# First attention's tail: SyncE issues all loads, the last x goes straight to its place, scatters begin between the last heads, no shared unit in the routing

## What is computed

```python
h  = cond_attn(x, fside, mask)            # layernorm, 16 heads over 513 keys, causal, bias, layernorm
x1 = x + head_mix(h)                      # per token: softmax over the 16 heads of the same token, @ Wout + bout
# mixture of experts with 8 experts, top 2, and a shared expert
scores = softmax((x1 @ wt.T + g @ wg.T) / 2)
w, idx = top_k(scores, 2)
y  = sum_k(w_k * expert[idx_k](x1)) + (leaky(x1 @ sw_gate) * (x1 @ sw_up)) @ sw_down
out = x1 + ffn(y)                         # a second attention, layernorms, and a mixture with 8 experts, top 1
```

## Time and profile before

| What | Value |
|---|---|
| median of 3 runs | 2566.62 us (2559.79 to 2570.12) |
| the profiled execution's own time | 2564.33 us |
| its span, first to last instruction | 2562.5 us |
| mean granted TensorE clock | 0.935 |
| busy share: PE, DVE, ACT, POOL | 83%, 58%, 46%, 40% |
| DMA, mean | 68 GB/s |

### The profile page before, as it was taken

How to read it: one execution, slowest core, us unless ns; L and a number is a source line. 1 busy time by engine, 2 the same in 40 slices (tenths; PEclk the granted TensorE clock), 3 DMA queues, 4 the chain that set the end, 5 groups by cost and what they waited for, 6 DMA issues and landing times.

```text
span 2562.5 us, 33680 instructions
## 1 busy us (share of the span) xinstructions
PE 2136.9 (83%) x11656; PEld 1152.8 (45%) x11656; DVE 1483.5 (58%) x3123; ACT 1174.8 (46%) x2748; POOL 1015.0 (40%) x790
## 2 busy tenths in 40 slices
PE   2999999999898988855857948899999988835995
PEld 1555555555555655522426823233333323313764
DVE  1346767786868686758423437666676664313336
ACT  0776666666666665611112421455555545401221
POOL 0105656574747484733365521102221011243216
PEclk9999999999999999978888977999999999857998
DMA  7002222221100000020434522111111502014214
GB/s 234 10 34 78 79 80 79 70 87 66 58 18 10 10 5 13 5 87 1 129 127 150 157 82 59 41 32 54 44 54 38 183 17 71 17 41 144 64 53 134
DMA packets 149647, 173.98 MB, mean 68 GB/s; under 512 B 18633, under 2 KB 132809, under 8 KB 149226
## 3 DMA queue, kind: packets, MB, share of 16 engines
q1 hardware_dynamic: 85226, 81.32, 10.2%
q10 hardware_dynamic: 49712, 50.79, 5.8%
q0 software_dynamic: 14544, 39.73, 5.0%
HBM read 86.98 MB, written 80.61 MB: 65 GB/s over the span
## 4 chain that ended last, share of the span: by engine, by line
PE 58%; POOL 12%; DVE 11%; ACT 8%; issue 5%; ACTq 2%; DMA 2%; SPq 1%; POOLq 0%; DVEq 0%
PE ps L1767 11%; POOL prod L815 7%; ACT m_pt L1895 6%; PE ps L574 3%; PE ps L547 3%; PE ps L533 3%; PE ps L558 3%; PE ps L584 3%; PE ps L2111 3%; PE ps L2119 3%; PE ps L1778 3%; DVE sc L827 3%; PE ps L1733 3%; DVE pb L698 2%; PE ps L1211 2%
## 5 line engine op out<-in xcount | busy, mean ns | idle before, releaser
L1832 DVE TENSOR_REDUCE m_mx<-ps 128x2 f32<-128x1024 f32 x256 | 312.4, 1224 | 178.2 <-PE ps L1751 177.2
L1895 ACT ACTIVATE m_pt<-ps 128x1024 f32<-128x1024 f32 x256 | 262.0, 1023 | 310.0 <-PE ps L1767 310.0
L698 DVE CUSTOM_DVE_ANT_0 pb<-ps,bias,snl 128x128 f32<-128x128 f32 (+3 forms) x512 | 260.4, 546 | 226.4 <-PE ps L547 223.6
L815 POOL TENSOR_TENSOR prod<-qs,kvs 128x1024 f32<-128x1024 f32 x120 | 285.1, 2403 | 224.9 <-issue 132.8
L1767 PE MATMUL ps<-m_q,m_k 32*128 32x512 f32 x1024 | 294.3, 651 | 52.2 <-ACT m_pt L1895 44.0
L815 POOL TENSOR_TENSOR prod<-sc,kvs 128x1024 f32<-128x1024 f32 x120 | 280.8, 2373 | 112.5 <-ACT sc L933 91.3
L1751 PE MATMUL ps<-m_k,m_q 32*128 32x512 f32 x1024 | 290.1, 666 | 5.2 <-DVE m_mx L1832 5.1
L893 ACT ACTIVATE pb<-pb,mst 128x129 f32<-128x129 f32 (+3 forms) x512 | 283.4, 560 | 21.1 <-DVE mst L698 19.1
L547 PE MATMUL ps<-kz,qT 64*128 64x128 f32 (+3 forms) x1024 | 185.3, 440 | 0.0
L558 PE MATMUL ps<-ident,pb 128*128 128x128 f32 x1280 | 180.0, 280 | 0.5 <-DVE mst L698 0.4
L1914 POOL DMA_INDIRECT m_yg<-ye_scratch,e_pos x64 | 63.4, 991 | 284.4 <-DVE m_x L1820 248.1
(11 more groups left out here) (326 smaller groups left out, 3773.9 us busy)
## 6 DMA issues: line engine op xcount, KB each, us to landing
xe_scratch<-zt ACTq DMA_DIRECT2D x32, 1024.0 KB, 4.5
ye_scratch<-e_ys SPq DMA_DIRECT2D x36, 256.0 KB, 2.1
hw_w<-in_w SPq DMA_DIRECT2D x16, 512.0 KB, 5.7
ys_scratch<-h_ys SPq DMA_DIRECT2D x39, 128.0 KB, 1.7
xin<-in_x SPq DMA_DIRECT2D x8, 512.0 KB, 3.6
bias<-in_fside ACTq DMA_DIRECT2D x8, 512.0 KB, 11.6
xr<-in_x SPq DMA_DIRECT2D x32, 128.0 KB, 2.3
y_scratch<-e_y SPq DMA_DIRECT2D x8, 512.0 KB, 3.2
```

The costliest lines, as they stand in the source:

```text
L698: dv.tensor_tensor_reduce(pb.ap[:, j, SEG[t]:SEG[t] + n], rS.of(("S", b, p, t, j)).ap[:, 0:n], k.bias[:, h, CAUSAL[t]:CAUSAL[t + 1]], -1.0 ...
L815: e.tensor_tensor(out, one, two, ALU.mult).then_inc(*k.c.did(*product_done(step, b, t, u)))
L1832: dv.tensor_reduce(x.ap[:, t, 64 * half:64 * half + 64].rearrange("p (i r) -> p i r", i=2)[:, :, 16], k.qS.of((b, g, t, half)).ap, AX, ALU ...
L1895: ac.activation(p.ap[:, 2 * half:2 * half + 2, :], k.qE.of((b, g, kt, half)).ap, ACT.Exp).then_inc(*did("m_exp", b, g, kt, half))
```

## The change

SP takes over all loads that ACT issued in `e_weights` and `mha_load`. A new step `x_last`, right behind `e_weights`, loads the four x tiles of batch 7 straight into their places in `e_x`; POOL adds the bias to all four at once, and `turn_o` of batch 7 no longer loads or adds on SP and POOL; `x1` adds in place. `e_load` stands before the heads `two` instead of behind them. In `two` there are nine shared units (n = 0, 1, 2, 4, 5, 6, 8, 9, 10) instead of six (n = 0, 2, 4, 6, 8, 10), and one tile's scatters behind n = 7 and behind n = 9. In batch 7's routing one shared unit is left instead of five, before its `count`. The transposes and scores of batch 7 use the PSUM banks of the ring `rM`.

```diff
+        elif step == "x_last":
+            for t in range(NT):
+                sp.dma_start(x1_tile(k, NB - 1, t), ins["x"][NB - 1, t * P:(t + 1) * P, :]).then_inc(*did("d_xl", t))
+        elif step == "turn_o" and key[0] < NB - 1:
...
-            x = k.xr.of((b, t))
+            x = x1_tile(k, b, t)
             w.wait_ge(at("wout", b, t), at("xb", b, t))
-            dv.tensor_tensor(x1_tile(k, b, t), rM.of(("x1", b, t)).ap[:, 0:D], x.ap[:, :], ALU.add).then_inc(*did("x1", b, t))
+            dv.tensor_tensor(x, rM.of(("x1", b, t)).ap[:, 0:D], x, ALU.add).then_inc(*did("x1", b, t))
...
+        elif step == "x_last":
+            w.wait_ge(at("d_xl", NT - 1))
+            for t in range(NT):
+                x = x1_tile(k, NB - 1, t)
+                po.tensor_tensor(x, x, k.bout[:, :], ALU.add).then_inc(*did("xb", NB - 1, t))
...
-    out = [("e_weights",)] + [x for part in start for x in part]
+    rows = [("scatter", n) for n in range(*LOT[0])]
+    share = iter([("shared", i) for i in range(2 * NB + 2)])
+    out = [("e_weights",), ("x_last",)] + [x for part in start for x in part]
...
-    out += turns
-    chain, i = routes(0), 0
+    out += turns + [("e_load",)]
+    chain = routes(0)
     for n, part in enumerate(two):
         out += part + chain[:1]
         chain = chain[1:]
-        if n % 2 == 0:
-            out.append(("shared", i))
-            i += 1
-    out += chain + [("e_load",)]
+        if n % 4 != 3:
+            out.append(next(share))
+        if n > 6 and n % 2:
+            out.append(rows.pop(0))
+    out += chain
     for part in end:
-        out += part + [("shared", i)]
-        i += 1
-    out += [("scatter", n) for n in range(*LOT[0])]
+        out += part + [next(share)]
+    out += rows
     b = NB - 1
-    for x in [("r_turn", b), ("r_score", b), ("r_back", b)] + routes(1):
-        out.append(x)
-        if x[0] in ("r_turn", "r_back", "r_soft", "r_rank", "r_cnt"):
-            out.append(("shared", i))
-            i += 1
-    return out + [("scatter", n) for n in range(*LOT[1])] + [("slots",)] + [("shared", j) for j in range(i, 2 * NB + 2)]
+    out += [("r_turn", b), ("r_score", b), ("r_back", b)] + routes(1)[:-1] + [next(share), ("count", 1)]
+    return out + [("scatter", n) for n in range(*LOT[1])] + [("slots",)] + list(share)
...
+def route_ring(k, b):
+
+    return k.rR if b < NB - 1 else k.rM
...
 def sync_two(k, sp, w, order):
...
+    def load(name, i, dst, src):
+        sp.dma_start(dst, src).then_inc(*did("d_" + name, i))
...
 def scalar_two(k, ac, w, order):
...
-    def load(name, i, dst, src):
-        ac.dma_start(dst, src).then_inc(*did("d_" + name, i))
...
-ONE = frozenset("turn_h lat q2 kv2 hs hs_soft hs_sum hv hv_end turn_o x1".split())
+ONE = frozenset("x_last turn_h lat q2 kv2 hs hs_soft hs_sum hv hv_end turn_o x1".split())
```

More of the change, by code:

```diff
@@ L969, in gpsimd_one @@
                 product(k, po, w, step, b, t, u)
-        elif step == "turn_o":
+        elif step == "x_last":
[3 more added lines that the diff above has]
+                po.tensor_tensor(x, x, k.bout[:, :], ALU.add).then_inc(*did("xb", NB - 1, t))
+        elif step == "turn_o" and key[0] < NB - 1:
             b, t = key
@@ L1095, in pairs_of @@
     return slice(2 * j * P, 2 * (j + 1) * P)
+def route_ring(k, b):
+    return k.rR if b < NB - 1 else k.rM
 def sync_two(k, sp, w, order):
     did, ins = k.c.did, k.ins
+    def load(name, i, dst, src):
+        sp.dma_start(dst, src).then_inc(*did("d_" + name, i))
     for step, *key in order:
-        if step == "e_load":
+        if step == "e_weights":
+            load("router", 0, cols(k.wt), ins["moe_wt"].rearrange("(c p) e -> p c e", p=P))
+            load("router", 1, cols(k.wg), ins["moe_wg"])
+            load("router", 2, cols(k.cT), ins["condT"][:, 0:NB])
+            load("router", 3, cols(k.before), ins["c_before"])
+            for b in range(NB - 1):
+                w.wait_ge([at(f"d_x1_{t % 2}", b, t) for t in range(NT)])
+                load(f"ex1_{b}", 0, k.ex1[:, b * NT:(b + 1) * NT, :], k.x1d[b * NT:(b + 1) * NT].rearrange("t p d -> p t d"))
+            load("shared", 0, cols(k.sg), ins["sh_gate"].rearrange("(c p) m -> p c m", p=P))
+            load("shared", 1, cols(k.su), ins["sh_up"].rearrange("(c p) m -> p c m", p=P))
+            load("shared", 2, cols(k.sd), ins["sh_down"].rearrange("(c p) m -> p c m", p=P))
+            load("tables", 0, cols(k.upper), ins["c_upper"])
+            load("tables", 1, cols(k.thr), ins["c_thr"][:, 0:2 * NN])
+            load("tables", 2, cols(k.iota), ins["c_iota"][:, 0:NS_E])
+            load("tables", 3, cols(k.place), ins["c_place"])
+        elif step == "mha_load":
+            load("mw", 0, cols(k.mwqk), ins["wi_qk"].rearrange("(c p) n -> p c n", p=P))
+            load("mw", 7, cols(k.mwv), ins["wi_v"].rearrange("(c p) n -> p c n", p=P))
+            load("mw", 1, cols(k.mbqk), ins["bi_qk"])
+            load("mw", 2, cols(k.mbv), row(ins["bi"][2 * D:3 * D]))
+            load("mw", 3, cols(k.mwo), ins["wo2"].rearrange("(c p) n -> p c n", p=P))
+            load("mw", 4, cols(k.mbo), row(ins["bo2"]))
+            load("mw", 5, cols(k.mg1), row(ins["ln1_g"]))
+            load("mw", 6, cols(k.mb1), row(ins["ln1_b"]))
+            w.wait_ge(at("d_yd0", 0))
+            load("m_x0", 0, cols(k.mx), k.yd[0:NT].rearrange("t p d -> p t d"))
+        elif step == "e_load":
             for x in range(E8):
@@ L1138, in tensor_two @@
             b = key[0]
-            m = k.rR.take(("score", b), at("e_lgT", b))
+            m = route_ring(k, b).take(("score", b), at("e_lgT", b))
             w.wait_ge(at("e_xT", b, 1), at("d_router", 3), m.room)
@@ L1437, in scalar_two @@
 def scalar_two(k, ac, w, order):
-    did, ins = k.c.did, k.ins
-    def load(name, i, dst, src):
-        ac.dma_start(dst, src).then_inc(*did("d_" + name, i))
+    did = k.c.did
     for step, *key in order:
[L1444 to L1459, removed]
+        if step == "r_init":
             w.wait_ge(at("e_cs", 0))
@@ L1465, in scalar_two @@
                 w.wait_ge(at("e_tr", b, c))
-                ac.activation(k.exT[:, b, c, :], k.rR.of(("turn", b, c)).ap, ACT.Copy).then_inc(*did("e_xT", b, c))
+                ac.activation(k.exT[:, b, c, :], route_ring(k, b).of(("turn", b, c)).ap, ACT.Copy).then_inc(*did("e_xT", b, c))
         elif step == "r_score":
@@ L1470, in scalar_two @@
             w.wait_ge(at("e_lg", b), at("e_csc", 0), l.room)
-            ac.activation(l.ap[:, :], k.rR.of(("score", b)).ap[0:E8, :], ACT.Identity, bias=k.cs[:, b:b + 1], scale=0.5).then_inc(*did("e_lgT", b))
+            ac.activation(l.ap[:, :], route_ring(k, b).of(("score", b)).ap[0:E8, :], ACT.Identity, bias=k.cs[:, b:b + 1], scale=0.5).then_inc(*did("e_lgT", b))
         elif step == "r_soft":
@@ L1489, in scalar_two @@
                                   ACT.Copy).then_inc(*did("sh_y", b, v))
[L1490 to L1500, removed]
         elif step == "expert":
```

3 lines of the change are left out of this document (1 added, 2 removed).

## The result

The changed kernel took 2545.6 us (median of 5 runs, 2539.37 to 2549.28) against 2566.62: a ratio of 0.9914, with the 95% interval 0.9892 to 0.9937. That is 22 us less (16 to 28), where the prediction said 26 less in its sum and 2540 us in its text. The profiled execution took 2549.28 us with a span of 2547.5.

The account below looks back on a forecast made before the run. The prediction took POOL's issuing of 64 scatters to end the stage before the second fence. Its terms, -27.2 - 2.8 + 2.6 + 4.0 - 2.8, summed to -26.2 us, giving 2540 us, range of 8 in 10 2530 to 2554.

Parts of the forecast that it names:

- (1): On POOL between its last product and the scatters: the wait for x and the bias adds go, -27.2 us.
- (2): Between POOL's `hv` products: the first tile's two scatters fit into its 14.06 us wait for DVE, -2.8 us.
- (3): Up to POOL's last product: DVE does the second half of five shared units instead of three, +2.6 us.
- (4): At `count`: unit 3's down projection ahead of it makes DVE wait longer for the counting matmuls, +4.0 us.
- (5): Start of the heads: hT comes earlier, but POOL's products must wait for `x_last`, so only -2.8 us.
- (6): Batch 7's routing: lot 1's positions come at about 1284, wanted at about 1307, so hidden by 23 us.
- (7): Start of part 2: nothing waits for SP's or ACT's queue when `mha_load` is on SP, 0.
- rival A: Scatters beside DVE stretched by the shared port: mild form costs 18 us, 2558 us, chance 0.07; slower 0.03.
- Rival B: Heads 6 us late as x lands with the expert loads, 10 to 13 with slow adds; 2550 to 2554; chance 0.10.
- Rival C: End of the stage: PE or DVE becomes the bound; PE losing 10 us gives 2549 us; chance 0.06.

Follow-up runs that it names:

- e13: The kernel before with only `x_last` added (x of batch 7 loaded straight to its place, bias added at once); 0.9919 of the kernel before, fence to fence 217.8 us.
- e1: The kernel before with only `e_load` moved ahead of the heads `two`; 0.9962 of the kernel before, fence to fence 240.0 us against 242.1.
- e4: The changed kernel with all scatters behind the heads, none between the last products; executed once, fence to fence 223.3 us against 218.7.
- e5: The changed kernel with six shared units in the heads `two` (n even) instead of nine; 0.9869 of the kernel before, fence to fence 211.5 us.
- e3: The changed kernel with `x_last` ahead of `e_weights`, so x of batch 7 loads first; 0.9874 of the kernel before, fence to fence 208.2 us.
- e6: The changed kernel with five shared units in batch 7's routing, as before the change; executed once, fence to fence 217.3 us against 218.7.
- after_again: The changed kernel run once more with no edit; 0.9914 of the kernel before, fence to fence 218.6 us.
- e12: The changed kernel with `e_weights` back on ACT and the expert loads behind the heads `two` again; executed once, fence to fence 222.0 us.
- e9: The changed kernel with `e_weights` back on ACT, nothing else; 0.9943 of the kernel before, fence to fence 227.9 us.

## Why the prediction was right

The sum said 26.2 us off the end of the scatters; the profile shows 23.4. By its own steps, each counted behind the fence:

(1) The hole. Right: it is gone, and e13 shows that it was the whole gain. The queue of SP and the ring of two buffers made it together; e1 took away only the queue's share, 12.0 of the 25.88 us of waiting. One reading in this step does not hold: the expert loads had all been issued by 1251.4, ahead of the first scatter at 1256.40, so the rows before say little about scatters beside them.

(2) Two scatters in POOL's wait. Right in that they fit: positions were ready at 1213.14, the products could start at 1219.26, and POOL still waited 3.33 us. The value of 2.8 us was not confirmed: e4 puts it at about 1 us, from one profile.

(3) and (4), more units ahead and `count` behind a down projection. DVE's wait grew by 2.95 us against 4.0 expected. e5 takes both away, and counted from q2 of tile 3 its bulk begins 5.6 us earlier: the wait's 2.95 and 2.65 for the two units, where 2.6 were expected.

(5) The start of the heads. Right in its mechanism and close in its numbers: POOL was free of `x_last`'s adds at 23.9 us behind the fence (expected 23.7). hT began 1.2 us behind the fence and the gain of it was lost on POOL, as e3 shows: 10.4 us of it come back when x is loaded first. q2 of tile 3 moved by 1.3 us instead of 2.8. Of the 1.5 missing, 1.0 is a product of DVE (1125.36) that took 2.19 us beside POOL's second product, where the next one took 1.21: POOL's product ended 28.5 us behind the fence as forecast, but DVE's sum of it began only at 29.5. The other 0.5 is PE, which came out of its wait at a granted clock of 0.50. It had done so before too, behind 5.68 us, but now four matmuls of the next turn took 2.32 us where they had taken 1.88. The prediction had not asked what PE would do while POOL waited.

Together (1) and (3) to (5) put the bulk 23.73 us ahead of the old first scatter; the prediction's figures (1256.4 and 1232.7) make 23.7. That they agree so closely is luck: (5) gave 1.5 us less than forecast, (4) cost 1.05 less, and from q2 of tile 3 to the last product the heads are 0.7 us shorter in e5, which has the same six units, than before; nobody had counted that.

(6) and (7). Lot 1's positions were there at 177.4 us and wanted at 206.2: hidden, and e6 shows it with 19 us less of cover. `mha_load` on SP cost nothing at the start of part 2: ACT's first copy there followed PE's transposes as before. What it does to the rest of part 2 to 5 is told only within the 5 us given at after_again.

What was missed is the row of scatters itself: 62 of them took 88.0 us from first to last start, where 64 had taken 87.8. This is the mechanism of rival A, but on three scatters of the row and not on all 62. Two of the stretched ones stand where DVE ran a product or a comparison on two SBUF operands: the scatter at 1229.08 took 1.96 us beside the product at 1228.99, that of 1275.57 took 1.47 beside the comparison at 1275.51. The scatter at 1226.28, which had begun ahead of the product at 1226.73, kept its 0.96 us. The Trainium skill, in SBUF — State Buffer, Who interferes with whom, says that a DVE instruction with two SBUF inputs contends with a GpSimd instruction that reads SBUF: the trace agrees. The same section infers that such a product would not hold up the generation of a DMA's descriptors; by these rows the scatter instruction was longer all the same. Against the row before, the stretching costs 1.6 us here, not the 18 of the rival. Another 1.5 us is in waits that come every 14 scatters and took up to 3.23 us (1304.14) instead of 2.1; what lengthens those was not tried by itself. Together they are what the two scatters of (2) were to give.

Rival B's range had a slip: with both slow adds, 10 to 13 us late, its gain would be 10 to 13 us, not 13. Rival B did not come true, as x was there 21.15 us behind the fence, where 20.9 were forecast. Rival C was judged wrongly in size: the prediction had PE's end within 2 to 6 us of POOL's, it was 14 us ahead of it (201.5 and 0.6 against 216.0). This is why the change's nine units were a loss: there was room for six.

The gain of 23.4 us in one stretch is a ratio of 0.9909 of the kernel, inside the interval measured. The prediction's 2540 was 5.6 us low; 2.8 of these are the tail, the rest is less than the spread of the runs.

## What to carry to other kernels

When an engine stands still ahead of the row of work that ends a stage, look at what is queued in front of the transfer it waits for: loading four small tiles straight to their place at the start of the stage gave all that the whole change gave. A load that somebody waits for goes ahead of the bulk in its queue, and moving bulk loads to another queue pays only if the first wait behind them moves with them. Work that fills an idle engine is not free if its second half runs on the engine that sets the pace.

## What the runs showed that was not expected

Loads of a second queue at the same time slow a queue's issuing: ACT's 18 loads took 14.5 us (14.9 in e12) with SP nearly silent, 21.1 us beside 24 loads of SP in e1, and 19.5 us in e9. The granted clock of TensorE stood at 0.50 behind PE's wait in the heads, whether that was 17 us or the 5.68 us of before, and the same four matmuls then took 3.58, 2.32 or 1.88 us in different executions. And the stretch ahead of the first fence took 1095.5 to 1107.2 us in these profiles, the one behind the tail 1214.7 to 1234.5, whatever the kernel.
